# A two-layer cross-attention and mixture-of-experts kernel: attention as straight code, one ring entry for maxima and outputs, stage borders reordered

## The chip, the core and the metric

The kernel runs on one core of one Trainium2 chip. The metric is the time of one execution on the device, in microseconds (us). Its engines are TensorE (PE; PEld is its weight load), VectorE (DVE), ScalarE (ACT), GpSimd (POOL) and SyncE (SP), which here only issues DMAs and waits.

## The reference

Four batches of 512 tokens with 512 features (x), and a context of 512 tokens with 128 features for each batch. Two layers, each of two residual steps with a gate:

```python
x = x + tanh(g_xattn[l]) * attention(layernorm(x), ctx, ctx)   # 32 query heads, 8 kv heads, D = 16
x = x + tanh(g_ffn[l]) * ffn(layernorm(x))
# attention: softmax(q k^T / 4) v, four query heads share a kv head, no projections
# ffn, layer 0: 8 experts of width 256, top 2 by softmax, and a shared expert of width 1024
# ffn, layer 1: 32 experts of width 192, top 6 by sigmoid, and a shared expert of width 384
# an expert: (silu(x wg) * (x wu)) wd; the chosen ones' weights are normalized to sum 1
```

All is float32. The kernel gets its precision on TensorE from splitting each operand into a high and a low part in a shorter type (names in `_hi`, `_lo`, `_parts`) and adding three products.

## The kernel before

x stays in SBUF for the whole program (16 tiles of 128 tokens, L50 and L580 share it). The stages follow each other: attention of layer 0 (0 to 479 us), FFN of layer 0 (to 1042), attention of layer 1 (to 1512), FFN of layer 1 (to 2289). Each stage is a block in which every engine runs its own program, written out by hand, with semaphores between them.

**Attention** (make_attention, L50). A *unit* is one kv head of one batch: 32 units. Each engine has a `step(b, k)`, and `steps` (L100) runs it for batch 0 as straight code, for batches 1 to 3 in a hardware loop (`Fori`), and for four more steps that drain the pipeline. In step n the maxima of unit n - 1 are taken, the negated maxima of n - 2 are turned and placed, unit n - 3 is exponentiated and multiplied by v, and the output of n - 4 is turned and scaled.

- The scores are computed twice. Once (score_for_max, L354) with tokens of x on the partitions: 16 blocks of 128 x 512 for a unit, of which VectorE takes the row maxima (take_max, L528). Then (score_for_exp, L369) with context on the partitions, where one row of the weights holds the maximum, which comes with the product; ScalarE takes the exponential, and probs_times_v (L388) multiplies by v and a column of ones.
- Three PSUM banks, `ring_ps`, are shared in turn (RING_ORDER, RING_BANK, L36 to L47) by 16 score blocks ("max"), the turned maxima ("neg", turn_max L331), the turned x of a later head pair ("q", turn_q L319, odd steps only) and the turned output ("out", turn_out L341). An entry may be written when the one three places before it has been read (ring_bank_free, L296).
- Maxima: POOL splits them in high and low (split_max, L236), TensorE turns them in four transposes of 8 columns, ScalarE copies 8 rows of 512 (copy_max, L443), SyncE places them by DMA in `q_turned` (place_max, L181). The output is copied by ScalarE (copy_out), turned by four transposes, divided by its sum on VectorE (scale_out, L541, after maximum 14) and added to x by POOL.
- Operands of the score matmuls are laid out by SyncE: place (L156) issues seven DMAs for a unit: three parts of k, three of q, and a tile of "no maximum". It waits first for the split of k and of q.
- For each batch VectorE takes mean and variance (moments, L485), subtracts k_hi from the context (split_k, L515) and normalizes (L498). Moments and split_k of batches 1 to 3 stand at the head of steps 1 to 3 of batch 0; the normalization stands among the maxima of step 4 of the batch before (next_batch, L505). POOL has the inverse root (root). In the last four steps the moments for the FFN are taken, a batch each.
- Loads at the start: x of batch 0 in one DMA, the whole transposed context in one, two gates, the context by tokens, and x of batches 1 to 3, all from SyncE (L140 to L154).

**FFN** (make_ffn, L580). VectorE takes the last moments, normalizes 16 tiles (L1281), SyncE stores them as rows in DRAM. A router chooses experts; VectorE makes the entries of a table (one pass for each chosen expert k, L1366 to L1371), then 35 small operations for the schedule (L1373 to L1414). TensorE then runs the shared expert in four groups of 512 tokens: for each of FC blocks of its width a gate/up phase (L969), then a down phase (L996), with y added to x by VectorE (L1492). Between its matmuls it makes the table by one-hot matmuls (L948; tile_hot by VectorE, tile_one_hots L1428, slot_hot by POOL, L813), over a ring of HOTS buffers (three in layer 1, four in layer 0). finish_table (L1445) reads it. Then the routed experts: POOL gathers 128 tokens at a time by indirect DMA (gather, L832), indexed by rows_in (VectorE, L1517), TensorE turns them (turn_x, L1016), multiplies with the expert's weights, and the results are scattered and added. Before: gathers 0 and 1 come after the schedule was read back, ScalarE's first rounding of expert weights after the last y (L1243), and the first expert's low parts (gu_lo) after the table.

The order of the work is that of these hand-written programs. An engine that waits holds back all that stands behind the wait in its program.

## Time and profile before

| | us |
|---|---|
| median of three runs | 2295.39 (2292.28 to 2306.82) |
| the profiled execution | 2291.02 |
| its span | 2289.3 |
| mean granted TensorE clock | 0.958 |
| attention of layer 0, of layer 1 | 479, 470 |
| FFN of layer 0, of layer 1 | 563, 777 |

The stage times are read off the timeline. The span is from the first to the last instruction of the profiled execution; the metric lies 1.7 us above it there. Busy time counts instructions only, not waits. In a timeline row the bracket holds the idle time ahead of it and the instruction that ended it.

### The profile page before, as it was taken

The numbers are of one execution on the slowest core, as the hardware profiler recorded it, in microseconds if no ns is written. First come the engines' busy times: TensorE is split into PE (matmuls) and PEld (weight loads), VectorE is DVE, ScalarE is ACT, GpSimd is POOL, SyncE is SP. The second block draws the span as 40 slices with busy tenths as digits, with TensorE's granted clock in tenths as the row PEclk, the third lists the DMA queues.
The fourth block names the chain that finished last, engine by engine and source line by source line (L and its number), as shares of the span: only waits on it lengthen the run. The fifth ranks groups of instructions, "written<-read, shape, count | busy, mean of one in ns | idle before, by whom it ended". The sixth has DMA issues, their size and how long they took to land. (4 is left out here: it accounts for less than half of the span.)

```text
span 2289.3 us, 42900 instructions
## 1 busy us (share of the span) xinstructions
PE 1990.7 (87%) x10024; PEld 1202.6 (53%) x10025; DVE 1349.5 (59%) x2607; ACT 1114.5 (49%) x1741; POOL 737.8 (32%) x856
## 2 busy tenths in 40 slices
PE   3899999979999979992899999976887998999997
PEld 1333333334666748871333333333555887878776
DVE  5888788833234324433888888838664454454443
ACT  1677676741212215540477777752113555565554
POOL 3111121121201015553121112122662554555555
PEclk9999999999999989995799999998998999999998
DMA  5222222141000037755122222140004787788785
GB/s 166 55 63 53 52 60 56 41 178 44 19 19 1 19 110 180 165 106 176 46 59 60 58 52 57 46 146 10 28 19 132 177 186 176 178 194 192 170 190 102
DMA packets 127292, 219.56 MB, mean 96 GB/s; under 512 B 16738, under 2 KB 58724, under 8 KB 126948
## 3 DMA queue, kind: packets, MB, share of 16 engines
q1 hardware_dynamic: 93412, 138.80, 20.7%
q0 software_dynamic: 33792, 79.71, 17.3%
q8 instruction: 40, 0.66, 0.1%
q14 instruction: 48, 0.39, 0.1%
HBM read 114.64 MB, written 56.63 MB: 75 GB/s over the span
## 5 line engine op out<-in xcount | busy, mean ns | idle before, releaser
L539 DVE TENSOR_REDUCE maxima<-ring_ps 128x1 f32<-128x512 f32 x1024 | 651.7, 685 | 150.3 <-PE ring_ps L366 138.7
L457 ACT ACTIVATE probs<-score_ps 128x1024 f32<-128x1024 f32 x512 | 497.1, 1018 | 79.9 <-PE score_ps L383 78.2
L366 PE MATMUL ring_ps<-k_turned,q_turned 64*128 64x512 f32 x1024 | 427.1, 488 | 95.7 <-DVE maxima L539 51.6
L366 PEld LDWEIGHTS ring_ps<-k_turned,q_turned 64*128 64x128 f32 x1024 | 180.6, 194 | 419.7 <-DVE maxima L539 267.1
L1028 PE MATMUL bank_f<-w_gu_parts_f,xg_T_f 128*128 x1800 | 371.2, 355 | 0.4 <-issue 0.4
L1028 PEld LDWEIGHTS bank_f<-w_gu_parts_f,xg_T_f 128*128 128x128 f32 x1800 | 330.5, 192 | 29.0 <-issue 1.3
L383 PE MATMUL score_ps<-q_turned,k_turned 64*128 64x512 f32 x1024 | 331.1, 450 | 1.6 <-ACT probs L457 1.4
L398 PE MATMUL out_ps<-probs,v_ones 128*32 128x512 f32 x2048 | 278.0, 615 | 0.5
L836 POOL DMA_INDIRECT xg_f<-xh_rows_f,idx_in_f x156 | 159.0, 1019 | 305.1 <-DVE idx_in_f L1517 204.5
L1053 PE MATMUL bank_f<-w_dn_parts_f,hg_T_f 96*128 (+1 forms) x888 | 244.2, 411 | 2.6 <-DVE hg_T_f L1529 1.4
L969 PE MATMUL bank_f<-x_parts_f,w_sh_parts_f 128*128 128x512 f32 x792 | 205.0, 400 | 13.6 <-DVE w_sh_parts_f L1442 13.6
L852 POOL DMA_INDIRECT out_x<-y_tok_f,idx_out_f x111 | 184.1, 1658 | 88.0 <-ACT y_tok_f L1225 36.7
L969 PEld LDWEIGHTS bank_f<-x_parts_f,w_sh_parts_f 128*128 128x128 f32 x792 | 148.8, 190 | 46.7 <-issue 16.3
L1053 PEld LDWEIGHTS bank_f<-w_dn_parts_f,hg_T_f 96*128 96x128 f32 (+1 forms) x888 | 157.9, 190 | 28.7 <-issue 3.4
L267 POOL TENSOR_TENSOR x_res<-x_res,scaled 128x256 f32 (+1 forms) x64 | 47.0, 734 | 390.0 <-DVE scaled L551 389.8
L996 PE MATMUL bank_f<-w_sh_down_f,h_T_f 128*128 128x512 f32 x352 | 156.8, 594 | 12.9 <-DVE h_T_f L1472 7.6
L813 POOL TENSOR_SCALAR slot_hot_f<-count_f_f,slot_of_f 128x128 fp32r<-128x128 f32 x128 | 101.9, 803 | 203.0 <-PE bank_f L948 201.9
L1537 DVE TENSOR_TENSOR h_tok_f<-silu_g_f,bank_f 128x192 f32<-128x192 f32 (+1 forms) x148 | 54.5, 368 | 188.6 <-ACT silu_g_f L1215 170.2
L383 PEld LDWEIGHTS score_ps<-q_turned,k_turned 64*128 64x128 f32 x1024 | 144.8, 190 | 25.1 <-ACT probs L457 13.6
L1016 PE MATMUL bank_f<-ident,xg_f 128*128 128x128 f32 x608 | 96.4, 282 | 55.1 <-DMA xg_f<-xh_rows_f,idx_in_f 51.8
L1505 DVE TENSOR_TENSOR w_gu_parts_f<-w_gu_f,w_gu_parts_f (+2 forms) x80 | 80.6, 1012 | 86.2 <-ACT w_gu_parts_f L1187 86.2
L253 POOL CAST q_hi<-q_raw 128x512 fp32r<-128x512 f32 x36 | 22.1, 613 | 291.7 <-ACT q_raw L438 178.0
(206 smaller groups left out, 2213.2 us busy)
## 6 DMA issues: line engine op xcount, KB each, us to landing
q_turned<-q_hi SPq DMA_DIRECT2D x128, 128.0 KB, 2.6
w_gu_f<-in_L_ffn_wg SPq DMA_DIRECT2D x32, 384.0 KB
w_gu_f<-in_L_ffn_wu SPq DMA_DIRECT2D x32, 384.0 KB
w_dn_f<-in_L_ffn_wd SPq DMA_DIRECT2D x32, 384.0 KB
k_turned<-k_hi SPq DMA_DIRECT2D x128, 64.0 KB, 2.1
q_turned<-q_lo SPq DMA_DIRECT2D x64, 128.0 KB, 2.6
q_turned<-no_max SPq DMA_DIRECT2D x64, 128.0 KB, 2.6
xh_rows_f<-xh_f SPq DMA_DIRECT2D x8, 1024.0 KB, 9.6
```

Of the source, the lines that this page charges most:

```text
L366: pe.matmul(ring(k, "max", i), q_turned[rows, slot, h // 2, c * P:(c + 1) * P], k_turned[rows, slot, :], start=True, stop=True).then_inc(m ...
L383: mm = pe.matmul(score_ps[:, pair, a, :], k_turned[rows, slot, c * P:(c + 1) * P], q_turned[rows, slot, pair, :], start=True, stop=True)
L398: mm = pe.matmul(out_ps[32 * h:32 * h + 32, :], v_ones[:, (k - LAG_EXP) % RING, c, :], probs[:, c % 2, h // 2, h % 2, :], start=(c == 0), ...
L457: act.activation(probs[:, c % 2, pair, :, :], score_ps[:, pair, :, :], ACT.Exp, scale=float(D) ** -0.5).then_inc(exped, 1)
L539: dve.tensor_reduce(maxima[:, par, c, col:col + 1], ring(k, "max", i), AX.X, ALU.max).then_inc(max_taken, 1)
L813: pool.tensor_scalar(slot_hot[:, n % HOTS, :], count_f[:], slot_of[:, i, k:k + 1], None, ALU.is_equal).then_inc(slot_hot_made, 1)
L836: pool.indirect_dma_start(xg[:, half, :], None, xh_rows, bass.IndirectOffsetOnAxis(ap=idx_in[:, half:half + 1], axis=0)).then_inc(gathered ...
L852: pool.indirect_dma_start(acc_rows, bass.IndirectOffsetOnAxis(ap=idx_out[:, half:half + 1], axis=0), y_tok[:, half, :], None, compute_op=A ...
L969: mm = pe.matmul(bank[:, 2 * (n % NBK) + o, :], w_sh_parts[:, o, w_part, d, :], x_parts[:, x_part, d, :], start=(d == 0 and j == 0), stop= ...
L996: mm = pe.matmul(bank[:, 6 + c % 2, :], h_T[:, f, c * P:(c + 1) * P], w_sh_down[:, f, :], start=(f == 0), stop=(f == FC - 1))
L1028: mm = pe.matmul(bank[:, half, 0:2 * F], xg_T[:, half, x_part, d, :], w_gu_parts[:, bass.ds(par, 1), w_part, d, :].rearrange("p a f -> p ( ...
L1053: mm = pe.matmul(bank[:, 2 + half, :], hg_T[:, half, h_part, f, :], w_dn_parts[:, bass.ds(par, 1), w_part, f, :].rearrange("p a f -> p (a ...
```

## The change

1. `steps` is straight code for all four batches in both layers; the bank of the last ring entry is no longer set by hand; the last batch does nothing for a batch behind it.
2. Moments and split_k of the next batch move from the head of steps 1 to 3 of batch 0 into the steps 1 (bn_stats), 2 (aggregates) and 3 (halves of split_k) of every batch but the last, between maxima. POOL's root goes to step 2.
3. "neg" and "out" become one ring entry, "turn", in the place of "neg". The 32 rows of maxima are turned by one transpose; the output by four matmuls that have it as weights and a 0/1 tile `pick` of 68 columns as moving operand, so that only the 17 columns in use of each head come out. VectorE, not ScalarE, copies the maxima (32 x 128 instead of 8 x 512), and scales after maximum 6 instead of 14. Each of the two placing DMAs takes 16 rows of 128 instead of 4 rows of 512.
4. At the start of attention x(0) is loaded by tiles, the context by batches (four DMAs in turn with x), gates by ScalarE's queue. ScalarE rounds only k of batch 0 before the first copies of q. The second q is split by VectorE instead of POOL. SyncE places k and "no maximum" first, and q after its wait.
5. FFN, start: tiles 0 to 3 are normalized before the moments of the last batch.
6. FFN, VectorE: passes 4 and 5 over the chosen experts (layer 1) come after the shared parts, the schedule operations are spread over the updates of x in groups 1 and 2, and one-hots are made two further ahead in the gate/up phases.
7. Border to the routed experts: the first two gathers are issued when the table is there; ScalarE's rounding waits for the split of the shared weights and the last h, not for the last y; gu_lo(0) stands before the last updates of x; TensorE waits for the last update only before turn_h(0); SyncE loads the next expert's weights before the last store. For that w_sh_down of layer 1 gets its own memory.

```diff
-TURN_NEG_AT, TURN_Q_AT, TURN_OUT_AT, SCALE_AT = 2, 5, 6, 14
-COPY_OUT_AT, COPY_NEG_AT, COPY_Q_AT = 1, 3, 6
+USED = D + 1
+TURN_AT, TURN_Q_AT, SCALE_AT = 2, 5, 6
+COPY_OUT_AT, COPY_Q_AT = 1, 6
...
-order += [("neg", 0)] * (d == TURN_NEG_AT) + [("q", 0)] * (d == TURN_Q_AT and k % 2) + [("out", 0)] * (d == TURN_OUT_AT)
+order += [("turn", 0)] * (d == TURN_AT) + [("q", 0)] * (d == TURN_Q_AT and k % 2)
...
-RING_BANK[RING_ORDER[-1]] = 1
...
-def steps(eng, step):
...
-    for k in range(KVH):
-        step(0, k)
-    with eng.Fori(1, B) as b:
+def steps(step):
...
+    for b in range(B):
...
+    def load_ctx_T(b):
+        sp.dma_start(ctx_T[:, :, b * S:(b + 1) * S], t["ctx_T"][:, :, b * S:(b + 1) * S]).then_inc(ctx_T_loaded[b], 16)
...
-    load_x(0)
-    sp.dma_start(ctx_T[:], t["ctx_T"]).then_inc(ctx_T_loaded, 16)
-    for i, g in enumerate((t["g_xattn"], t["g_ffn"])):
-        sp.dma_start(gate_raw[:, i:i + 1], g[layer:layer + 1].rearrange("(a n) -> a n", a=1).to_broadcast([P, 1])
-                     ).then_inc(gate_loaded, 16)
-    sp.dma_start(ctx_tok[:], t["ctx"].rearrange("b (n p) d -> p (b n) d", p=P)).then_inc(ctx_loaded, 16)
-    for b in range(1, B):
-        load_x(b)
+    for c in range(TPB):
+        sp.dma_start(x[:, c, :], t["x_rows"][c * P:(c + 1) * P, :]).then_inc(x_first[c], 16)
+    for b in range(B):
+        load_ctx_T(b)
+        if b == 0:
+            sp.dma_start(ctx_tok[:], t["ctx"].rearrange("b (n p) d -> p (b n) d", p=P)).then_inc(ctx_loaded, 16)
+        else:
+            load_x(b)
...
-        sp.wait_ge(k_lo_made, b + 1)
-        sp.nop(nofuse=True)
-        sp.wait_ge(q_split, b * (KVH // 2) + (2 * (k // 4) + 2))
+        sp.wait_ge(k_lo_made, 2 * b + 2)
...
+        sp.dma_start(q_turned[3:P:4, k, :, :].bitcast(F32), no_max[:]).then_inc(placed[k % 2], 16)
+        sp.wait_ge(q_split, b * (KVH // 2) + (2 * (k // 4) + 1))
+        sp.nop(nofuse=True)
+        if (b, k) == (0, 0):
+            sp.wait_ge(second_q, 2)
+        sp.nop(nofuse=True)
...
-        sp.dma_start(q_turned[3:P:4, k, :, :].bitcast(F32), no_max[:]).then_inc(placed[k % 2], 16)
...
+    pool.memset(pick[:], 0.0).then_inc(picked, 1)
+    pool.wait_ge(picked, 1)
+    pool.affine_select(out=pick[:], in_=pick[:], compare_op=ALU.not_equal, fill=1.0, base=0,
+                       pattern=[[-P // G, G], [-1, USED]], channel_multiplier=1).then_inc(picked, 1)
...
-            elif what == "neg":
+            elif what == "turn":
+                if (u := stage(b0, k0, LAG_OUT)) is not None:
+                    pe.wait_ge(out_read, u + 1)
...
-                    return pe.wait_ge(max_copied, u + 1)
-            elif what == "out":
-                if (u := stage(b0, k0, LAG_OUT)) is not None:
-                    return pe.wait_ge(out_read, u + 1)
-            elif not isinstance(b0, int) or -3 <= b0 * KVH + k0 < UNITS:
+                    pe.wait_ge(max_copied, u + 1)
+                if u is not None or stage(b0, k0, LAG_OUT) is not None:
+                    return
+            elif -3 <= b0 * KVH + k0 < UNITS - 3:
...
-        ring_bank_free(b, k, "neg")
-        for c in range(TPB):
-            mm = pe.transpose(ring(k, "neg")[0:2 * G, c * P:(c + 1) * P].bitcast(F32R),
-                              max_parts[:, (k - LAG_NEG) % 2, c, :], ident_r[:])
-        mm.then_inc(max_turned, 1)
+        ring_bank_free(b, k, "turn")
+        pe.transpose(ring(k, "turn")[0:2 * SLOTS, SLOTS * USED:SLOTS * USED + P].bitcast(F32R),
+                     max_parts[:, (k - LAG_NEG) % 2, :], ident_r[:]).then_inc(max_turned, 1)
...
-        ring_bank_free(b, k, "out")
+        if stage(b, k, LAG_NEG) is None:
+            ring_bank_free(b, k, "turn")
+        if isinstance(b, int) and u == 0:
+            pe.wait_ge(picked, 2)
...
-            mm = pe.transpose(ring(k, "out")[:, c * P:(c + 1) * P], out_rows[:, c * P:(c + 1) * P], ident[:])
+            mm = pe.matmul(ring(k, "turn")[:, c * G * USED:(c + 1) * G * USED], out_rows[:, c * P:(c + 1) * P],
+                           pick[:].rearrange("p h e -> p (h e)"), start=True, stop=True)
...
                 probs_times_v(b, k, c)
-            if d == TURN_NEG_AT:
+            if d == TURN_AT:
                 turn_max(b, k)
+                turn_out(b, k)
             if d == TURN_Q_AT:
                 turn_q(b, k)
-            if d == TURN_OUT_AT:
-                turn_out(b, k)
...
+    round_k(0)
     copy_q(-1, 5)
     copy_q(-1, 7)
-    steps(act, step)
+    for b in range(1, B):
+        round_k(b)
+    steps(step)
...
+    def next_batch(b, k, n):
...
-        if rest:
-            return
-        if c == 0:
-            dve.wait_ge(ln_rstd, B)
-            dve.wait_ge(q_turns, b * (KVH // 2) + KVH // 2)
-        normalize(b + 1 if isinstance(b, int) else (b + 1) % B, c)
...
-    def split_k(b):
+        if b + 1 >= B or rest:
+            return
+        if k == 1:
+            if c == 0:
+                dve.wait_ge(x_loaded[b + 1], 16)
+            moments_of_tile(b + 1, c)
+        elif k == 2 and c == 0:
+            moments_of_batch(b + 1)
+        elif k == 3 and c < 2:
+            split_k(b + 1, c)
+        elif k == KVH // 2:
+            if c == 0:
+                dve.wait_ge(ln_rstd, b + 2)
+                dve.wait_ge(q_turns, b * (KVH // 2) + KVH // 2)
+            normalize(b + 1, c)
...
+    def split_k(b, half):
...
-        dve.tensor_tensor(k_lo[:, :, cols], ctx_T[:, :, cols], k_hi[:, :, cols].bitcast(F32), ALU.subtract
+        dve.tensor_tensor(k_lo[:, half, cols], ctx_T[:, half, cols], k_hi[:, half, cols].bitcast(F32), ALU.subtract
...
-    dve.wait_ge(x_loaded[0], 16)
-    moments(0)
+    def split_second_q():
...
+        dve.wait_ge(q_copied, 2)
+        dve.tensor_copy(q_hi[:, 0, 1, :], q_raw[:, 1, :]).then_inc(second_q, 1)
+        dve.wait_ge(second_q, 1)
+        dve.tensor_tensor(q_lo[:, 0, 1, :], q_raw[:, 1, :], q_hi[:, 0, 1, :].bitcast(F32), ALU.subtract).then_inc(second_q, 1)
...
+    for c in range(TPB):
+        dve.wait_ge(x_first[c], 16)
+        moments_of_tile(0, c)
+    moments_of_batch(0)
...
-    split_k(0)
+    for half in range(2):
+        split_k(0, half)
+    split_second_q()
...
+    def copy_max(b, k):
+        if (u := stage(b, k, LAG_NEG)) is None:
+            return
+        par = (k - LAG_NEG) % 2
+        dve.wait_ge(max_turned, u + 1)
+        if (out := stage(b, k, LAG_OUT)) is not None:
+            dve.wait_ge(out_turned, out + 1)
+        if past(b, k, LAG_NEG + 2):
...
+            dve.wait_ge(max_placed[par], 16 * u + (0 if par == 0 else -16))
+        dve.tensor_copy(max_rows[:, par, :], ring(k, "turn")[0:2 * SLOTS, SLOTS * USED:SLOTS * USED + P]
+                        ).then_inc(max_copied, 1)
...
-        turned_out = ring(k, "out").rearrange("p (c h e) -> p (c h) e", c=TPB, h=G)
+        turned_out = ring(k, "turn")[:, 0:SLOTS * USED].rearrange("p (n e) -> p n e", n=SLOTS)
...
     def step(b, k):
-        if isinstance(b, int) and b == 0 and 0 < k < B:
-            dve.wait_ge(x_loaded[k], 16)
-            moments(k)
-            split_k(k)
-        if isinstance(b, int) and b == B and k >= 1:
+        if b == B and k >= 1:
             dve.wait_ge(x_added, KVH * k)
-            moments(k - 1, B)
+            for c in range(TPB):
+                moments_of_tile(k - 1, c)
+            moments_of_batch(k - 1, B)
         for n in range(SLOTS):
...
             if n == SCALE_AT:
+                copy_max(b, k)
                 scale_out(b, k)
-            if k == KVH // 2:
-                next_batch(b, n)
-    steps(dve, step)
+            next_batch(b, k, n)
+    steps(step)
     dve.wait_ge(x_added, UNITS)
...
+        if b == B - 1:
...
+            sp.wait_ge(expert_w, 48)
+            sp.wait_ge(hot_used, PAIRS)
+            load_expert(1, 1)
...
-    sp.wait_ge(expert_w, 48)
-    sp.wait_ge(hot_used, PAIRS)
-    load_expert(1, 1)
...
+    gather(0, 0)
+    gather(1, 1)
...
-    for i in range(7):
-        if i >= 2:
-            pool.wait_ge(xg_turned, i - 1)
+    for i in range(2, 7):
+        pool.wait_ge(xg_turned, i - 1)
...
     turns = pe.value_load(turns_i[0:1, 0:1], min_val=4, max_val=64)
+    pe.wait_ge(y_read, TT - 1)
     turn_x(0, 0)
...
     gate_up(1, 1, expert_of(1))
+    pe.wait_ge(y_read, TT)
     turn_h(0, 0)
...
-    act.wait_ge(y_done, TT)
+    act.wait_ge(sw_split, 2 * (B - 1) * FC)
+    act.wait_ge(h_done, B * FC)
     gu_hi(0, 0)
     gu_hi(0, 1)
+    if layer == 0:
+        act.wait_ge(y_done, TT)
     dn_hi(0)
...
+    for i in range(TPB):
+        normalize(i)
...
-    for k in range(K):
+    def weights_of(k):
...
+        dve.wait_ge(table_ready, 1)
+        rows_in(0, 0)
+        rows_in(1, 1)
+    for k in range(min(K, 4)):
+        weights_of(k)
     shared_x_lo(1)
...
     shared_w_lo(FC, 1)
+    for k in range(4, K):
+        weights_of(k)
     for n in range(FC, B * FC):
...
             used = hots_by(g, (f * 2 + o + 1) * HC * 3)
-            tile_one_hots(used)
+            tile_one_hots(used + (2 if f + 1 < FC else 0))
             if f + 1 < FC:
                 shared_w_lo(n + 1, o)
-        if f + 1 < FC:
-            tile_one_hots(used + HOTS // 2)
         dve.wait_ge(silu_done, n + 1)
...
+        if g + 1 == B:
+            gu_lo(0, 0)
+            gu_lo(0, 1)
...
+            if (g, c) == (1, 0):
+                experts_ended()
+            if (g, c) == (1, 1):
+                next_expert()
+            if (g, c) == (1, 2):
+                schedule_of()
+            if (g, c) == (1, 3):
+                turn_counts()
+            if (g, c) == (2, 0):
+                last_tokens()
+            if (g, c) == (2, 1):
+                first_tokens()
+            if (g, c) == (2, 2):
+                experts_meet()
+            if (g, c) == (2, 3):
+                landing_counts()
```

## Rows read from the trace of the kernel before

In a fence, "..." stands where lines of the answer are left out.

**Rows 1.** The page, parts 1 and 2: busy time of each engine, and TensorE's granted clock.

```profile
PE 1990.7 (87%) x10024; PEld 1202.6 (53%) x10025; DVE 1349.5 (59%) x2607; ACT 1114.5 (49%) x1741; POOL 737.8 (32%) x856
...
PEclk9999999999999989995799999998998999999998
```

**Rows 2.** Windows: busy (count) of PE, PEld, DVE, ACT, POOL; granted clock; DMA share; GB/s.

```profile
140.00:200.00 60.00, 57.34 (x353) 22.48 (x352) 53.19 (x92) 43.29 (x51) 10.59 (x24) 1.00 0.25 62
...
234.00:236.00 2.00, 2.00 (x10) 1.16 (x7) 0.00 (x0) 0.74 (x2) 0.00 (x1) 0.50 0.49 110
...
22.00:24.00 2.00, 0.00 (x0) 0.00 (x0) 0.00 (x0) 0.00 (x0) 2.00 (x2) 1.00 1.04 383
```

**Rows 3.** Timeline of VectorE, the scaling once a step: start us, busy us, engine, line, operation.

```profile
156.62 0.42 DVE L551 TENSOR_TENSOR scaled<-ring_ps,recip 128x256 f32<-128x256 f32 x1
...
168.60 0.42 DVE L551 TENSOR_TENSOR scaled<-ring_ps,recip 128x256 f32<-128x256 f32 x1
...
181.40 0.42 DVE L551 TENSOR_TENSOR scaled<-ring_ps,recip 128x256 f32<-128x256 f32 x1
...
194.44 0.42 DVE L551 TENSOR_TENSOR scaled<-ring_ps,recip 128x256 f32<-128x256 f32 x1
...
231.81 0.42 DVE L551 TENSOR_TENSOR scaled<-ring_ps,recip 128x256 f32<-128x256 f32 x1
...
250.59 0.42 DVE L551 TENSOR_TENSOR scaled<-ring_ps,recip 128x256 f32<-128x256 f32 x1
...
1273.12 0.42 DVE L551 TENSOR_TENSOR scaled<-ring_ps,recip 128x256 f32<-128x256 f32 x1
...
1287.89 0.43 DVE L551 TENSOR_TENSOR scaled<-ring_ps,recip 128x256 f32<-128x256 f32 x1
```

**Rows 4.** Timeline of TensorE, FFN layers; in brackets idle time before and who ended it.

```profile
839.41 1.12 PE L1016 MATMUL bank_f<-ident,xg_f 128*128 128x128 f32 x4 [10.12 <-DMA xg_f<-xh_rows_f,idx_in_f]
...
1600.06 1.62 PE L969 MATMUL bank_f<-x_parts_f,w_sh_parts_f 128*128 128x512 f32 x3 [13.61 <-DVE w_sh_parts_f L1442]
...
1612.78 0.41 PE L948 MATMUL bank_f<-tile_hot_f,slot_hot_f 128*128 128x384 f32 x1 [1.21 <-DVE tile_hot_f L1421]
...
1740.13 1.11 PE L1016 MATMUL bank_f<-ident,xg_f 128*128 128x128 f32 x4 [8.76 <-DMA xg_f<-xh_rows_f,idx_in_f]
```

**Rows 5.** Timeline of VectorE, the filling of batch 0 in layer 0.

```profile
32.90 2.46 DVE L489 BATCH_NORM_STATS2 stats<-x_res 128x6 f32<-128x512 f32 x4
...
35.89 1.22 DVE L518 TENSOR_TENSOR k_lo<-ctx_T,k_hi 128x1024 fp32r<-128x1024 f32 x1
```

**Rows 6.** Timeline of TensorE, attention of layer 0.

```profile
29.29 0.79 PE L366 MATMUL ring_ps<-k_turned,q_turned 64*128 64x512 f32 x2 [13.19 <-DMA q_turned<-no_max]
...
254.46 0.41 PE L337 MATMUL ring_ps<-ident_r,max_parts 128*8 128x128 f32 x4
...
255.08 0.50 PE L366 MATMUL ring_ps<-k_turned,q_turned 64*128 64x512 f32 x1 [0.21 <-DVE maxima L539]
...
261.22 0.66 PE L347 MATMUL ring_ps<-ident,out_rows 128*128 128x128 f32 x4
```

**Rows 7.** Groups of instructions by line: busy us, mean ns, idle before and releaser.

```profile
L539 DVE TENSOR_REDUCE maxima<-ring_ps 128x1 f32<-128x512 f32 x1024 | 651.7, 685 | 150.3 <-PE ring_ps L366 138.7 <-issue 7.2
...
L813 POOL TENSOR_SCALAR slot_hot_f<-count_f_f,slot_of_f 128x128 fp32r<-128x128 f32 x128 | 101.9, 803 | 203.0 <-PE bank_f L948 201.9
```

**Rows 8.** Timeline of SyncE's queue at the start of attention, layer 0.

```profile
22.75 0.56 SPq L174 DMA_DIRECT2D k_turned<-k_hi  x1
...
26.54 0.60 SPq L179 DMA_DIRECT2D q_turned<-no_max  x1
```

**Rows 9.** Timeline of VectorE in the FFN of layer 1.

```profile
1526.48 1.92 DVE L1288 TENSOR_SCALAR xh_f<-x_res,mean_var,rstd 128x512 f32<-128x512 f32 x4 [7.02 <-DMA xh_rows_f<-xh_f]
...
1586.77 0.18 DVE L1373 CAST ends_i_f<-ends_f_f 128x32 int32<-128x32 f32 x1
...
1597.02 2.28 DVE L1436 TENSOR_TENSOR x_parts_f<-xT_f,x_parts_f 128x2048 fp32r<-128x2048 f32 x1
```

202 lines of the change are left out of this document (103 added, 99 removed).

## Prediction

> **What bounds the kernel now.** I read the page's busy times first. TensorE is busy for 87% of the span and VectorE for 59%, and the granted clock is near full in all but a few slices [rows 1]. So TensorE bounds the kernel, and time can be won only in two ways: give it less to do, or close gaps in it. Next come the windows by stage. In the steady part of an attention layer TensorE is busy for 57.34 of 60 us [rows 2], so 4% is there to win by scheduling. At the edge of the attention loop it runs at half the clock, 0.50 (the 1.2 GHz level), after a pause in which all engines stood still [rows 2]. Then I timed a step (one kv head of one batch) by the spacing of the "scaled" instruction on VectorE: 11.98 us for a plain step, 13.04 us for one with four normalizations among its maxima, 18.78 us at a loop edge of layer 0 and 14.77 us at one of layer 1 [rows 3]. In the FFN layers the gaps stand in the timeline of TensorE: one of 13.61 us before the first shared group of layer 1, small ones of 1.21 us at the table's one-hots, and one of 10.12 and of 8.76 us at the border from shared to routed experts [rows 4]. Two layers, so most items count twice.
>
> **Edges of the loop.** Batches 1 to 3 run in a loop of TensorE, VectorE, ScalarE, POOL and SP; straight code takes its place. Each layer has two jumps back and an exit. In layer 0 the jumps cost 18.78 - 11.98 = 6.8 us each (two of them, alike within 0.01), and the entry and tail another 2.5 together: 16.1. In layer 1 the first jump takes 14.77 [rows 3] and the second is shorter: 2.8 and 1.4, with entry and tail 2.5: 6.7. I take these back in full, **-22**. Below: with the slow-clock microseconds after each pause [rows 2] also back, -28. Above: 0, if straight code stalls for its own instructions. That jumps of one loop differ from 1.4 to 6.8 speaks for a stall of instruction loading, and in straight code the next instructions can be fetched ahead of use.
> The Trainium skill (Runtime: NRT & Kernel Launch, section Instruction fetch mechanics) says that prefetch is purely sequential and that a taken branch outside the loaded window forces a stall. The trace's loop edges agree with it in place; by that rule the term is -22 too.
>
> **The filling of batch 0.** In the first three steps VectorE does a lump before its first maximum: four bn_stats, 2.46 us, four aggregates and a sum, 0.55, and the k_lo subtraction of 1.22, about 4.1 us [rows 5] (of it 0.4 of small waits); TensorE has nothing queued past the three ring banks, so it stands. Three lumps cost the layer some 9.5 us of TensorE time (three times 4.1 less what the filling hid). Spread among the maxima, the same work costs what four normalizations of 0.54 cost today: 13.04 - 11.98 = 1.06 per step [rows 3]. It now falls in batches 0, 1 and 2: statistics in step 1 (+1.3), aggregates in step 2 (+0.3), halves of k_lo in step 3 (+0.5), so +1.9 to 2.1 a batch. For batch 0 that is inside the 9.5; for batches 1 and 2 it is new. -9.5 + 3.9 = -5.6 a layer, **-11**. Bounds -19 (spread work hidden under maxima's waits for TensorE) and 0.
>
> **One ring entry for maxima and outputs.** Today a step has a maxima turn of 0.41 and an output turn of 0.66 overlapping to 0.59, with small waits of 0.21 behind the former [rows 6], so 1.0 of PE time and about 0.3 of stalls. After: one transpose, 0.10, and four fp32 matmuls of 68 columns with the rows as weights. Each is two passes as the 128-column form is (0.66 for four [rows 6]), so 0.14 to 0.21 for each of four: 0.56 to 0.86. Work falls by about 0.3 to 0.5. Against that, one entry of three banks now holds a bank until maximum 6 is read (0.68 [rows 7]), a copy (an estimate of 0.23, half of the 0.42 of the scaling [rows 3], for half the columns), a reciprocal of the same size and the scaling are done: 0.9 us of VectorE in a row where there was 0.7, plus handing over of 0.25. The maximum that wants this bank then waits 0.3 to 0.5. Net I take -0.2 a step, 56 steps: **-11**. The new wait, for both turns, has all later maxima of VectorE behind it, and behind those TensorE; both turns end before maximum 5, so it should cost nothing. Bounds: -0.5 (-28) and +0.3 (+17). VectorE gains 0.23 a step and ScalarE loses 0.59; neither is the bound (53.19 and 43.29 of 60 [rows 2]), but VectorE comes nearer. The negated maxima land 8.7 us into a step: the copy ends at about 5.5, after six of sixteen maxima and the turn, SP issues for 0.56 [rows 8], and from an issue to the score that used it 2.7 us passed at the start (26.54 [rows 8] to 29.29 [rows 6]). They are wanted at about 9.4, where TensorE's first score for exp of that unit stands: hidden, with 0.7 of slack where there was 1.6.
>
> **No work for a fifth batch.** The last batch turns and normalizes nothing: four q turns and the four normalizations, 1.06 + 1.3, -2.4 a layer, **-5**. Bounds -6 and -3.
>
> **Start of attention.** The first score waits 13.19 us for the landing of the last placement [rows 6]: k parts are issued from 22.75 and no_max, the last, at 26.54 [rows 8]. Reordered, the q parts would be issued at about 17.6 (x by tiles, so that statistics, normalization, two turns and two splits start earlier, by as much as three of four tiles of the load). But the loads of x and ctx are still filling the DMA engines at 22 to 24 (383 GB/s [rows 2]) and end near 24.5. The placements, 704 KB, drain behind them in 1.8 us, plus 1 of latency: 27.3 instead of 29.3, **-4** for two layers. Bounds: at once, 17.6 + 2.7 = 20.3, -9 a layer (-18); and +2 a layer, if ctx in smaller pieces (2 KB for 8) makes the loads longer.
> The Trainium skill (DMA: Bandwidth & Descriptors, section Queues, rings and completion order) says that on each DMA engine the descriptors of one issuer's ring are consumed in order. It speaks against this edit: placements issued early stand behind SP's loads. By it the term is -4; without it, -18. No row of before shows a placement issued while a load of the same queue was still waiting.
>
> **Start of the FFN.** Four normalizations move ahead of the last batch's moments. Today VectorE normalizes two batches after the moments and then waits 7.02 us for the stored rows, before four that take 1.92 [rows 9]. What precedes the store (variance, POOL's root, zeroing) is late by the 1.92 of four normalizations: +1.9 twice, **+4**. Bounds 0 (the pause swallows it) and +4.
>
> **Schedule arithmetic of layer 1.** 35 small VectorE instructions from 1586.77 to 1597.02, 10.25 us, stand ahead of the parts that the first shared group waits for [rows 9]. So do two groups of weights, which move only behind those parts (they take some 3 us, and the first one-hots come after them, in good time). They go into the down phases of groups 1 and 2. The gap of 13.61 shrinks by 10.25. But in a down phase VectorE must feed one-hots through a ring that holds three: 4.73 us of arithmetic in group 1 and 5.53 in group 2 come back as waits, 10.26. Net with a little clock **-1**. Bounds -14 (arithmetic hidden under the down phases) and +6. In layer 0 it is hidden before and after: 0.
>
> **One-hots ahead.** In layer 1 TensorE waits 1.21 us for a one-hot at each f border of the gate/up phases [rows 4]: four a group, three groups, 14.4. Asking for two more one-hots before hides nearly all: -13 in layer 1 and -1.3 in layer 0, **-14**. Bounds -16 and 0: POOL's share of a one-hot takes 0.80 us [rows 7], not far from the pace of use, so POOL may be next.
>
> **Borders.** The gathers of the first two tiles are issued from the table instead of after the schedule; gate/up weights no longer wait for the last y. The gaps of 10.12 and 8.76 us [rows 4] close to nothing, as the gather (flight near 7) then lies beside the last down phase: **-19**. Bounds -19 and -5 (the table's last one-hots come at the end of the phase, and some flight stays uncovered).
>
> **Sum.** -22 - 11 - 11 - 5 - 4 + 4 - 1 - 14 - 19 = -83. The profiled execution took 2291.0; 2291 - 83 = 2208. The median of the runs shown lies 4.4 above the profiled one: **2212**.
>
> **Rivals.** (1) The merged turn doesn't pay: VectorE's chain decides, +0.3 a step instead of -0.2: +28, 2240. For it: a chain of copy, reciprocal and scaling on an engine with 53 of 60 us used; against it: PE work falls. Chance 0.17. (2) Placements don't queue behind the loads: -14 more, 2198. For it: 2.7 us of flight in the steady part; against: 383 GB/s on the engines at that time. 0.12. (3) Straight code stalls at its own fetches as often as the loop did: the 22 are not won, 2234. 0.06. (4) Slower than before: the copy of the maxima, now behind both turns and behind maximum 6, makes the negatives land late and all score matmuls for exp wait. From +1.4 us in each of some 60 steps it eats the 83; at +1.6, where -0.2 stood, it gives 2212 + 1.8 x 56 = 2313. For it: slack falls from 1.6 to 0.7 us. Against: a lateness of over 2 us needs a flight of twice the 2.7 seen. 0.05. The forecast itself has 0.60.
>
> **How the numbers follow.** The main case's own range is 2185 to 2238 (its terms at half way to their bounds, signs mixed). To 2240 and 2198 it takes in rivals 1 to 3, and the bounds of the borders and the schedule (+14, -13) widen it to 2180 to 2250. A change of 1% is 23 us, about what a measurement of this kernel can tell from none. Faster by over 1% means under 2272: the main case and rivals 1 to 3 lie there, 0.90 with 0.05 off for a joint miss of several terms; that goes to "within". Slower is rival 4, 0.05.
>
> **What would show it.** Right: steps at 11.8 us (plain) without any of 14 to 18; the clock above 0.95 around 235 us; no lump of four bn_stats; the gap before the first shared group near 3.4, and new waits for one-hots of some 5 us each in the down phases of groups 1 and 2; no waits of 1.2 us at f borders; under 1 us at the borders; the first score at 27.3. The sum is wrong if plain steps are longer than 12.2 us, if TensorE waits for max_rows, or if POOL's one-hots become the releaser in the gate/up phases.

## The result and the profile after

The changed kernel takes 2231.69 us in the median (2225.11 to 2237.43), 0.9723 of the time before, with a 95% interval of 0.9694 to 0.9752. The forecast was 2212 in a range of 2180 to 2250: right in direction and inside the range, 20 us too low. Of the two profiled executions the span fell from 2289.3 to 2227.7, by 61.6 us, where the sum promised 83.

The page after, the lines that answer to [rows 1]:

```profile
PE 1987.7 (89%) x10072; PEld 1224.0 (55%) x10073; DVE 1357.3 (61%) x2675; ACT 1087.7 (49%) x1673; POOL 723.2 (32%) x848
...
PEclk9999999989999999995999999989999999999998
```

TensorE did the same work (1987.7 us against 1990.7) in a shorter span: what was won are gaps. The windows of the changed kernel, in the columns of [rows 2]:

```profile
140.00:200.00 60.00, 56.64 (x352) 23.58 (x348) 54.37 (x102) 41.41 (x46) 13.32 (x27) 1.00 0.25 63
...
232.00:244.00 12.00, 11.56 (x77) 5.07 (x73) 11.46 (x21) 7.57 (x9) 0.60 (x3) 1.00 0.25 61
```

The steady part didn't get denser: 56.64 of 60 us, where it was 57.34 [rows 2]. The stretch around the first former loop edge now runs at a granted clock of 1.00; from 232 to 244 us it was 0.67 before. The step, by the spacing of VectorE's scaling as in [rows 3]:

```profile
203.68 0.42 DVE L593 TENSOR_TENSOR scaled<-ring_ps,recip 128x256 f32<-128x256 f32 x1
...
215.69 0.43 DVE L593 TENSOR_TENSOR scaled<-ring_ps,recip 128x256 f32<-128x256 f32 x1
...
228.84 0.42 DVE L593 TENSOR_TENSOR scaled<-ring_ps,recip 128x256 f32<-128x256 f32 x1
```

A plain step takes 215.69 - 203.68 = 12.01 us, the next, with a q turn before its maximum 6, 228.84 - 215.69 = 13.15. A pair is 25.16, where before it was 24.62 (11.98 from [rows 3], and 12.64 for the step ahead of it, from the row at 143.98 shown below). TensorE in that stretch, and its first score:

```profile
29.01 1.22 PE L379 MATMUL ring_ps<-k_turned,q_turned 64*128 64x512 f32 x3 [14.18 <-DMA q_turned<-q_lo]
...
213.07 1.08 PE L359 MATMUL ring_ps<-pick,out_rows 128*128 128x68 f32 x8
...
216.17 0.49 PE L379 MATMUL ring_ps<-k_turned,q_turned 64*128 64x512 f32 x1 [0.37 <-DVE scaled L593]
...
221.13 0.50 PE L396 MATMUL score_ps<-q_turned,k_turned 64*128 64x512 f32 x2 [0.42 <-ACT probs L465]
```

Four output matmuls of 68 columns are eight passes that take 1.08 us, not 0.56 to 0.86; the four transposes of 128 columns in [rows 6] are four passes (x4), and not two each, as the prediction has it. The maximum behind the merged entry waits 0.37 us for the scaling. In the step with a q turn there is a new wait of 0.42 for ScalarE's exponential. The first score comes at 29.01, not at the 27.3 forecast. In the FFN layers, TensorE again:

```profile
806.94 0.60 PE L1060 MATMUL bank_f<-ident,xg_f 128*128 128x128 f32 x4
...
1547.92 0.66 PE L994 MATMUL bank_f<-tile_hot_f,slot_hot_f 128*128 128x384 f32 x1 [5.47 <-DVE tile_hot_f L1497]
...
1579.95 0.41 PE L994 MATMUL bank_f<-tile_hot_f,slot_hot_f 128*128 128x384 f32 x1 [2.81 <-DVE tile_hot_f L1497]
...
1624.75 0.41 PE L994 MATMUL bank_f<-tile_hot_f,slot_hot_f 128*128 128x384 f32 x1 [3.60 <-DVE tile_hot_f L1497]
...
1717.02 0.66 PE L1060 MATMUL bank_f<-ident,xg_f 128*128 128x128 f32 x4 [4.09 <-DMA xg_f<-xh_rows_f,idx_in_f]
```

At 806.94 (layer 0's border) the first turn has no wait any more; before it was 10.12 [rows 4]. Behind it TensorE now waits 2.72 us for VectorE's part of the turned rows (xg_T; 2.29 in layer 1), where it was 1.56. The first shared group of layer 1 now waits 5.47 us, for a one-hot, in the place of 13.61 [rows 4]. The longest waits for a one-hot in the down phases of groups 1 and 2 are 2.81 and 3.60. Before there was one in the same place, of 1.47 and 1.48:

```profile
1636.61 0.41 PE L948 MATMUL bank_f<-tile_hot_f,slot_hot_f 128*128 128x384 f32 x1 [1.47 <-DVE tile_hot_f L1421]
```

Added up over a down phase, these waits grew from 2.9 to 6.0 us in group 1 and from 2.9 to 8.2 in group 2. The waits of 1.2 at the f borders are gone. 4.09 us are spent waiting for a later gather.

**Where the 61.6 us went**, by the times at which the same TensorE instruction stands in both traces: the start of both attention layers gave 0.3 and 1.3; from the first score to the last turn of the maxima layer 0 fell from 431.1 to 407.9 and layer 1 from 421.6 to 408.2, so 36.6; the FFN starts cost 3.1 in layer 0 and gave 1.0 in layer 1; the shared groups gave 1.8 in layer 0 and 9.6 in layer 1; the borders gave 8.6 and 8.7, of which layer 1 returned 3.2 in its routed part. 1.6 + 36.6 - 2.1 + 11.4 + 14.1 = 61.6.

### The profile page after: what moved, and what is told of

Read it like the earlier page. It is cut to its first block and busy times, and to the rows that moved or that the text cites. A ratio compares the mean times of both kernels' runs of the same rounds, so it can differ in the third digit from the quotient of the medians.

```text
span 2227.7 us, 40122 instructions
## 1 busy us (share of the span) xinstructions
PE 1987.7 (89%) x10072; PEld 1224.0 (55%) x10073; DVE 1357.3 (61%) x2675; ACT 1087.7 (49%) x1673; POOL 723.2 (32%) x848
## 5 line engine op out<-in xcount | busy, mean ns | idle before, releaser
L465 ACT ACTIVATE probs<-score_ps 128x1024 f32<-128x1024 f32 x512 | 503.1, 1025 | 214.5 <-PE score_ps L396 212.5
L379 PE MATMUL ring_ps<-k_turned,q_turned 64*128 64x512 f32 x1024 | 412.8, 481 | 62.0 <-DMA q_turned<-q_lo 27.1
L1042 PE MATMUL bank_f<-w_sh_down_f,h_T_f 128*128 128x512 f32 x352 | 162.9, 613 | 12.6 <-DVE h_T_f L1567 7.6
L396 PEld LDWEIGHTS score_ps<-q_turned,k_turned 64*128 64x128 f32 x1024 | 149.6, 186 | 37.8 <-ACT probs L465 28.8
L278 POOL TENSOR_TENSOR x_res<-x_res,scaled 128x256 f32<-128x256 f32 x64 | 47.1, 735 | 240.1 <-DVE scaled L593 240.1
```

The costliest lines, as they stand in the source:

```text
L379: pe.matmul(ring(k, "max", i), q_turned[rows, slot, h // 2, c * P:(c + 1) * P], k_turned[rows, slot, :], start=True, stop=True).then_inc(m ...
L396: mm = pe.matmul(score_ps[:, pair, a, :], k_turned[rows, slot, c * P:(c + 1) * P], q_turned[rows, slot, pair, :], start=True, stop=True)
L465: act.activation(probs[:, c % 2, pair, :, :], score_ps[:, pair, :, :], ACT.Exp, scale=float(D) ** -0.5).then_inc(exped, 1)
L1042: mm = pe.matmul(bank[:, 6 + c % 2, :], h_T[:, f, c * P:(c + 1) * P], w_sh_down[:, f, :], start=(f == 0), stop=(f == FC - 1))
```

## The experiments

Times are medians; the ratio is to runs of the kernel before on the same chip. The changed kernel stands at 2231.69, 0.9723.

**straight_only.** The kernel before, with one part of the change.

```diff
-            for k in range(KVH):
-                step(0, k)
-            with eng.Fori(1, B) as b:
+            for b in range(B):
                 for k in range(KVH):
                     step(b, k)
```

> The kernel before with its attention loop written as straight code and nothing else changed (a batch that does not exist is still prepared). Theory (the loop's edges are instruction loading and registers): the steps at the edges, 18 us and 15 us, fall to those of the middle, the span falls by 22 us from 2289 to 2267. Rival (straight code stalls at its own fetches): under 5 us are won.

Measured 2287.49, ratio 0.9960 (0.9933 to 0.9986): 9 us, not 22. The trace tells why. TensorE at the first border of batches (a wait, then the turns of the maxima on either side of it, which lie 9 us before and 5 us after the wait):

```profile
131.35 0.49 PE L364 MATMUL ring_ps<-k_turned,q_turned 64*128 64x512 f32 x1 [1.13 <-DVE scaled L549]
...
122.11 0.41 PE L335 MATMUL ring_ps<-ident_r,max_parts 128*8 128x128 f32 x4
...
136.13 0.40 PE L335 MATMUL ring_ps<-ident_r,max_parts 128*8 128x128 f32 x4
```

From 122.11 to 136.13 is 14.02 us in straight code. The kernel before has the same wait at the same border, where no jump is, as it enters the loop:

```profile
131.06 0.50 PE L366 MATMUL ring_ps<-k_turned,q_turned 64*128 64x512 f32 x1 [1.14 <-DVE scaled L551]
```

In the prediction's own measure, VectorE's scaling, it shows as a step of 13.40 us at that border, 1.4 over the plain 11.98:

```profile
130.58 0.43 DVE L551 TENSOR_TENSOR scaled<-ring_ps,recip 128x256 f32<-128x256 f32 x1
...
143.98 0.42 DVE L551 TENSOR_TENSOR scaled<-ring_ps,recip 128x256 f32<-128x256 f32 x1
```

So of the 18.78 us at a loop edge 1.4 had nothing to do with the loop. In four of the eight borders of straight_only the granted clock also falls to 0.50 (1.2 GHz) behind this wait, and the step takes 15.10 to 15.18 us instead of 14.02. At the third border of layer 0:

```profile
336.00:338.00 2.00, 2.00 (x12) 1.32 (x8) 0.90 (x2) 1.07 (x2) 0.00 (x0) 0.50 0.59 139
```

Layer 1 of the kernel before has no more than this at its jumps: its steps there take 15.35 us (with the clock at 0.50 behind the wait) and 13.96 by the turns of the maxima. Its loop cost nothing that these rows show. In layer 0 each jump cost some 5.2 us: the step over it and the one behind take 18.02 + 13.31 by the same turns, in straight code 14.02 + 12.07. The part that belongs to the loop is seen on VectorE at the first edge of the kernel before, an idle time that no other engine ends ("issue"):

```profile
239.08 3.08 DVE L539 TENSOR_REDUCE maxima<-ring_ps 128x1 f32<-128x512 f32 x5 [2.28 <-issue]
```

Straight code removed this one; neither expectation had the split right.

**ring_runs_on.** straight_only, with the three banks counted on from batch to batch.

```diff
-RING_BANK[RING_ORDER[-1]] = 1
+RING_LENGTH = len(RING_ORDER)
...
-            return ring_ps[:, RING_BANK[k, what, i], :]
+            return ring_ps[:, (RING_BANK[k, what, i] + b * RING_LENGTH) % 3, :]
...
-                    if RING_BANK[k0, what, i] != RING_BANK[RING_ORDER[at]]:
+                    if back % 3:
```

> The kernel of straight_only with the ring's banks counted on through the batches, so that every entry reuses the bank of the entry three before it; before, the order of 148 entries began anew in each batch with bank 0, and the last output stood in bank 1. Theory (TensorE's wait of 1.13 us for the scaling at each end of a batch comes from this wrap, not from the loop): the steps of 14.02 us fall to 12.65, eight of them, so the span falls by about 11 us against straight_only, and about 20 against the kernel before (0.991). Rival (what is left at the batch borders is instruction loading): as straight_only, 0.996.

Measured 2271.73, ratio 0.9887 (0.9828 to 0.9947), 16 us below straight_only, 17 by the ratios. The wait is gone, and the step over the border takes 134.63 - 121.97 = 12.66 us:

```profile
121.97 0.40 PE L335 MATMUL ring_ps<-ident_r,max_parts 128*8 128x128 f32 x4
...
134.63 0.40 PE L335 MATMUL ring_ps<-ident_r,max_parts 128*8 128x128 f32 x4
```

The theory holds, and the gain is larger than the 11 us that it named. Eight steps shorter by 1.36 give 10.9, and the four that lost 1.1 us each to the clock give another 4.6: no border step of this trace is over 12.67. The order of 148 entries began anew with each batch, and its last entry, maximum 15, was put by hand into bank 1, where the output two entries ahead of it still stood until VectorE's scaling. The merged entry takes the place of that output far from the end of the order; its 140 entries begin anew too, but there a bank is only waited for behind a maximum, and no such wait is left in the changed kernel. The change names it in half a sentence (the bank of the last entry is no longer set by hand), and the prediction gives it no term. Against sep_turns, below, which keeps that bank, three border steps a layer are shorter by 0.87 and the last by 1.4, which makes 8 us of the gain.

**sep_turns.** The changed kernel with two ring entries again.

```diff
-TURN_AT, TURN_Q_AT, SCALE_AT = 2, 5, 6
-COPY_OUT_AT, COPY_Q_AT = 1, 6
+TURN_NEG_AT, TURN_Q_AT, TURN_OUT_AT, SCALE_AT = 2, 5, 6, 14
+COPY_OUT_AT, COPY_NEG_AT, COPY_Q_AT = 1, 3, 6
```

(with the two turns, copy_max of ScalarE, 8 rows of 512, and bank 1 for the last entry as in the kernel before)

> The changed kernel with maxima and outputs turned in two ring entries again, the maxima copied by ScalarE, the scaling after maximum 14; all else as changed. Theory (the merged entry costs time): a pair of steps takes 24.65 us as before the change instead of 25.16, about 14 pairs a layer, so the span falls by about 14 us, to 2214. Rival (the prediction's term, merging gains 0.2 us a step): the span rises by 11 us, to 2239.

Measured 2246.40, ratio 0.9773 (0.9729 to 0.9818): 0.005 or 11 us slower than the changed kernel, as the prediction's term says and not as the theory made from the trace. The two intervals overlap, but the traces say the same: between the first and the last turn of the maxima the two layers take 17.2 us more, of which 6.1 fall on four steps with the clock at half, and 11.0 are left. Yet its steps are the faster ones (the turn of the maxima in the last batch):

```profile
363.15 0.41 PE L342 MATMUL ring_ps<-ident_r,max_parts 128*8 128x128 f32 x4
...
375.22 0.41 PE L342 MATMUL ring_ps<-ident_r,max_parts 128*8 128x128 f32 x4
...
387.89 0.40 PE L342 MATMUL ring_ps<-ident_r,max_parts 128*8 128x128 f32 x4
```

12.07 + 12.67 = 24.74 for a pair, 0.42 less than 25.16. What it loses is at the borders of batches, 14.02 there as above, and in the steps with statistics and normalization, which are 0.6 and 0.8 us longer; why these two are longer is not shown. Without the places where the clock dips in one of the traces, a batch in the middle takes 104.03 us here and 102.08 in the changed kernel.

**copy_q_later** and **scale_earlier**, each one number of the changed kernel.

```diff
-COPY_OUT_AT, COPY_Q_AT = 1, 6
+COPY_OUT_AT, COPY_Q_AT = 1, 7
```

> The changed kernel with ScalarE's copy of the turned q behind its exponential 7 instead of 6. Theory (the copy waits for the turn and holds back exponential 7, for which TensorE then waits 0.42 us): the step with a q turn takes 12.7 us instead of 13.15, the span falls by 10 to 12 us. Rival (VectorE's chain sets the step): the wait moves to the ring, no change.

Measured 2217.25, ratio 0.9639 (0.9597 to 0.9681): 14 us by the medians. ScalarE now has both exponentials behind it when the turned q comes:

```profile
217.43 1.94 ACT L465 ACTIVATE probs<-score_ps 128x1024 f32<-128x1024 f32 x2 [1.07 <-PE score_ps L396]
...
220.06 0.60 ACT L456 ACTIVATE q_raw<-ring_ps 128x512 f32<-128x512 f32 x1 [0.69 <-PE ring_ps L338]
```

The step with a q turn takes 12.59 instead of 13.15.

```diff
-TURN_AT, TURN_Q_AT, SCALE_AT = 2, 5, 6
+TURN_AT, TURN_Q_AT, SCALE_AT = 2, 5, 5
```

> The changed kernel with copy_max and scale_out of VectorE after maximum 5 instead of 6. Theory (VectorE stands 0.46 us before maximum 6 while the turn is done, and TensorE waits 0.35 us for the scaling behind it): the plain step falls from 12.01 to about 11.65, the span by some 18 us. Rival (the bank of the next maximum comes free later by as much, or VectorE waits for the turn itself): no change or slower.

Measured 2207.34, ratio 0.9589 (0.9544 to 0.9633): 24 us for one number. The plain step takes 11.58 instead of 12.01. The scaling ends before maximum 6 is read, in the time in which VectorE used to stand, and the score behind the merged entry has no wait:

```profile
200.69 0.42 DVE L593 TENSOR_TENSOR scaled<-ring_ps,recip 128x256 f32<-128x256 f32 x1
...
202.05 0.81 PE L379 MATMUL ring_ps<-k_turned,q_turned 64*128 64x512 f32 x2
```

So the forecast's doubt about the merged turn (VectorE's chain of copy, reciprocal and scaling holds the bank) was sound; the chain stood one maximum too late.

**lump_again.** The changed kernel with the moments at the head of steps 1 to 3 of batch 0.

```diff
             def step(b, k):
+                if b == 0 and 0 < k < B:
+                    dve.wait_ge(x_loaded[k], 16)
+                    for c in range(TPB):
+                        moments_of_tile(k, c)
+                    moments_of_batch(k)
+                    for half in range(2):
+                        split_k(k, half)
...
```

(the same pieces taken out of the later steps, and POOL's root with them)

> The changed kernel with the moments and the split of k of batches 1 to 3 at the head of steps 1 to 3 of batch 0 again. Theory of the prediction: 9.5 us a layer come back in batch 0, 3.9 are saved in the later ones, so the span rises by 11 us to 2239. Rival (the spread work is hidden among the maxima and costs next to nothing): it rises by 16 to 19 us.

Measured 2253.11, ratio 0.9798 (0.9739 to 0.9857): 21 us more by the medians, 17 by the ratios (the interval touches that of the changed kernel; the traces below are clear). The turns of unit 0, of unit 7 and of unit 15, first here, then in the changed kernel:

```profile
54.66 0.29 PE L347 MATMUL ring_ps<-ident_r,max_parts 128*32 128x128 f32 x1
...
147.90 0.23 PE L347 MATMUL ring_ps<-ident_r,max_parts 128*32 128x128 f32 x1
...
249.00 0.23 PE L347 MATMUL ring_ps<-ident_r,max_parts 128*32 128x128 f32 x1
```

```profile
48.58 0.29 PE L347 MATMUL ring_ps<-ident_r,max_parts 128*32 128x128 f32 x1
...
136.48 0.22 PE L347 MATMUL ring_ps<-ident_r,max_parts 128*32 128x128 f32 x1 [0.19 <-DVE maxima L568]
...
238.56 0.23 PE L347 MATMUL ring_ps<-ident_r,max_parts 128*32 128x128 f32 x1 [0.20 <-DVE maxima L568]
```

The first turn comes 6.1 us later, the next seven units take 5.3 more, so the lumps cost 11.4 a layer and not 9.5. The second batch takes 101.10 instead of 102.08: spreading costs 1.0 a batch and not 1.95. That the statistics fill VectorE's waits for scores is the likely reason, not shown by itself. The rival's size holds: 9.4 a layer.

**loads_later.** The changed kernel's loads moved.

```diff
-            for b in range(B):
-                load_ctx_T(b)
-                ...
-                    load_x(b)
+            load_ctx_T(0)
...
                 place_max(b, k)
+                if (b, k) == (0, 1):
+                    for later in range(1, B):
+                        load_ctx_T(later)
+                        load_x(later)
```

> The changed kernel with SyncE's loads of context and x of batches 1 to 3 issued behind the placements of units 0 and 1. Theory (placements are served in the order of issue behind the loads on the same queue, they land 7.5 us after their issue instead of 2.7): the first score comes at 23.5 us instead of 29.0, the span falls by about 5 us a layer, to 2217. Rival (the operands or the engines are late anyway): the first score stays near 29, no change; a second rival, that the batches behind come late: VectorE waits for x in step 1.

Measured 2235.32, ratio 0.9723 (0.9668 to 0.9779): no change. But the two rows of theory and second rival are both there. In the changed kernel SyncE issues the placements of unit 0 from 15.12 on, and the last at 21.48 (the second of two rows; the first is held for 3.14):

```profile
15.12 3.14 SPq L176 DMA_DIRECT2D k_turned<-k_hi  x1
...
21.48 0.59 SPq L185 DMA_DIRECT2D q_turned<-q_lo  x1
```

The first score stands at 29.01, 7.5 us behind. With the loads out of the way SyncE issues the last at 18.99, and TensorE starts 2.7 us later:

```profile
18.99 0.59 SPq L181 DMA_DIRECT2D q_turned<-q_lo  x1
```

```profile
21.68 1.22 PE L379 MATMUL ring_ps<-k_turned,q_turned 64*128 64x512 f32 x3 [6.67 <-DMA q_turned<-q_lo]
...
34.20 1.39 PE L379 MATMUL ring_ps<-k_turned,q_turned 64*128 64x512 f32 x2 [7.78 <-DVE maxima L568]
```

So placements do stand behind loads issued earlier on the same queue, by 4.8 us here. The packets show that they wait and are not merely slowed: those of 4,096 bytes, which in this stretch only the placements have, start at 25.09 in the changed kernel, though the first DMA that has them was issued at 19.57, and at 17.36 with the loads out of the way, 1.3 us after their issue at 16.11. This is what the Trainium skill (DMA: Bandwidth & Descriptors, section Queues, rings and completion order) says of descriptors in a ring, and the runs agree. SyncE itself is held too: its first placement takes 3.14 us to issue behind the loads, 0.54 without them. The 7.3 us won were then lost at once in step 1, where x of batch 1 is late:

```profile
32.86 0.69 DVE L496 BATCH_NORM_STATS2 stats<-x_res 128x6 f32<-128x512 f32 x1 [7.28 <-DMA x_res<-in_x]
```

**ffn_passes_later.** The changed kernel with two moves on VectorE.

```diff
-            for k in range(4, K):
-                weights_of(k)
             for n in range(FC, B * FC):
...
+                if f == FC - 1 and g < 3 and 3 + g < K:
+                    weights_of(3 + g)
                 dve.wait_ge(silu_done, n + 1)
...
+                    if (g, c) == (1, 0):
+                        experts_ended()
+                    ...
                     dve.wait_ge(y_done, TPB * g + c + 1)
```

> The changed kernel with the passes over the fifth and sixth chosen expert in the last gate/up phase of groups 1 and 2, and the pieces of the schedule ahead of VectorE's wait for y instead of behind the update. Theory (the one-hots come in the order of the chosen experts, so the first ones don't need these passes, for which TensorE now waits 5.47 us; the pieces fit into VectorE's waits of 1.4 us): the wait of 5.47 goes, those of 2.81 and 3.60 us fall by half, the span falls by 8 us to 2219. Rival (VectorE is the bound of these groups): the waits turn up at the f borders and the time stays.

Measured 2215.02, ratio 0.9641 (0.9587 to 0.9695): 17 us, where the theory had 8. TensorE at the first gate/up phase, and its waits in the two down phases:

```profile
1546.35 1.25 PE L1015 MATMUL bank_f<-x_parts_f,w_sh_parts_f 128*128 128x512 f32 x3
...
1577.48 0.41 PE L994 MATMUL bank_f<-tile_hot_f,slot_hot_f 128*128 128x384 f32 x1 [2.69 <-DVE tile_hot_f L1497]
...
1619.24 0.41 PE L994 MATMUL bank_f<-tile_hot_f,slot_hot_f 128*128 128x384 f32 x1 [3.42 <-DVE tile_hot_f L1497]
```

The wait of 5.47 is gone. The two in the down phases stayed, 2.69 and 3.42: VectorE makes the low part of x for the next group ahead of the one-hot, as it did in the kernel before (1.47), and a piece of the schedule still stands there too, five operations from 1574.91 to 1576.05 in group 1. The shorter waits behind these fell, and the sum over a down phase went from 6.0 to 4.3 and from 8.2 to 6.0.

Much of the rest is the clock. Windows of the second down phase (group 2), here and in the changed kernel:

```profile
1611.60:1634.50 22.90, 16.95 (x53) 9.40 (x54) 20.84 (x42) 1.70 (x3) 14.42 (x15) 1.00 0.05 16
```

```profile
1616.90:1645.00 28.10, 19.90 (x51) 10.63 (x52) 20.84 (x42) 2.09 (x3) 13.30 (x15) 0.88 0.00 1
```

Over the three shared groups the stretch takes 119.4 us instead of 135.3: 6.2 less of waits and 7.4 less of TensorE's busy time for the same instructions, at a granted clock of 0.99 instead of 0.92.

**border_again.** The changed kernel with the border as before (gathers after the schedule, the expert's weights after the last y, TensorE's wait ahead of the first turn).

```diff
-            gather(0, 0)
-            gather(1, 1)
             pool.wait_ge(sched_in, 16)
...
-            act.wait_ge(sw_split, 2 * (B - 1) * FC)
-            act.wait_ge(h_done, B * FC)
+            act.wait_ge(y_done, TT)
...
-            pe.wait_ge(y_read, TT - 1)
+            pe.wait_ge(y_read, TT)
...
```

> The changed kernel with the border to the routed experts as before: gathers 0 and 1 after the schedule, gate/up weights of the first expert after the last y and the table, TensorE's wait for the last update ahead of the first turn. (The store order of SyncE and the memory of w_sh_down stay changed.) Theory: the gaps of 10.1 and 8.8 us are back, of which the trace of the changed kernel saves 8.6 and 8.8, and a later gather of layer 1 gives 3.2 back to it; the span rises by 14 to 17 us, to 2243. Rival (the gathers are bound by the rows of the DMA engines over the whole stage): under 8 us.

Measured 2243.82, ratio 0.9761 (0.9713 to 0.9808): 12 us by the medians, 9 by the ratios, where the theory had 14 to 17. The intervals overlap; the waits are clear:

```profile
814.75 1.09 PE L1059 MATMUL bank_f<-ident,xg_f 128*128 128x128 f32 x4 [6.55 <-DMA xg_f<-xh_rows_f,idx_in_f]
...
1689.24 1.09 PE L1059 MATMUL bank_f<-ident,xg_f 128*128 128x128 f32 x4 [7.17 <-DMA xg_f<-xh_rows_f,idx_in_f]
```

6.55 and 7.17 us are waited for the first gather, less than the 10.12 and 8.76 of before; SyncE's changed order of stores stayed in, and whether the difference is due to it wasn't tried.

**best_a** is the changed kernel with scale_earlier, copy_q_later and ffn_passes_later, and with the loads so:

```diff
                 place_max(b, k)
+                if (b, k) == (0, 0):
+                    load_x(1)
+                if (b, k) == (0, 1):
+                    load_ctx_T(1)
+                    for later in range(2, B):
+                        load_ctx_T(later)
+                        load_x(later)
```

> The changed kernel with scale_earlier (scaling after maximum 5), copy_q_later, ffn_passes_later, and the loads: x of batch 1 behind the placement of unit 0, all others behind that of unit 1. Theory: -24 (scaling, measured), -17 (passes, measured), part of the -14 of the q copy (the same wait may be shared), -6 a layer from the start, as x of batch 1 no longer comes late: the span falls to about 2165 (ratio 0.945). Rival (the waits of scaling and q copy are one): 2180.

Measured 2175.14, ratio 0.9458 (0.9415 to 0.9502). TensorE has its first score at 21.73, and no wait for the maxima as long as the 7.78 of loads_later:

```profile
21.73 1.22 PE L382 MATMUL ring_ps<-k_turned,q_turned 64*128 64x512 f32 x3 [6.78 <-DMA q_turned<-q_lo]
...
27.27 1.39 PE L382 MATMUL ring_ps<-k_turned,q_turned 64*128 64x512 f32 x2 [0.79 <-DVE maxima L571]
```

A new wait came instead, of 3.42 us (4.56 in layer 1). ScalarE rounds k of batches 1 to 3 ahead of its first copy of q in the steps, and now waits for the last piece of the context:

```profile
37.43 1.06 ACT L448 ACTIVATE k_hi<-ctx_T 128x1024 fp32r<-128x1024 f32 x1 [3.11 <-DMA ctx_T<-in_ctx_T]
```

```profile
39.02 1.22 PE L382 MATMUL ring_ps<-k_turned,q_turned 64*128 64x512 f32 x3 [3.42 <-ACT q_raw L459]
```

The gains of the scaling and of the q copy nearly add: a plain step takes 11.58, one with a q turn 12.16.

**best_b** is best_a with the low part of x moved down.

```diff
                     tile_one_hots(used + HOTS)
-                    shared_x_lo(g + 1)
...
-                    if g + 1 < B and c < 2:
-                        shared_w_lo(n + 1, c)
+                    if g + 1 < B and c == 1:
+                        shared_x_lo(g + 1)
+                    if g + 1 < B and c >= 2:
+                        shared_w_lo(n + 1, c - 2)
```

> best_a with the low part of x of the next shared group and of its first weights made by VectorE among the second to fourth down column instead of before the first. Theory (TensorE waits 2.69 and 3.42 us for the one-hot behind that subtraction): -4 us against best_a. Rival (the subtraction is then late for the one-hots of the next columns): no change or slower.

Measured 2175.98, ratio 0.9469 (0.9417 to 0.9521): no change. TensorE's longest waits in the two down phases became 1.87 and 3.05, at the next column. The wait moved with the subtraction, as the rival has it.

## Why the prediction was right, and which steps of it were not

The total is in part luck: the loop was priced 13 us too high, the filling 6 to 10 too low, and the merged entry came to its number by other parts than those named.

- **Edges of the loop, -22: wrong step, measured -9.** The step that failed is to count all that a border has over 11.98 us as the loop's. By the scaling, the border into the loop took 13.40 without any jump, the wrap of the ring; the second jump of layer 1 took the same 13.40, and the first 14.77, the wrap with the clock at half behind it (straight code has 14.52 for that). So the 6.7 us of layer 1 were none of the loop's, and in layer 0 some 5.3 of the 6.8 a jump were. The prediction counted the wrap as entry and tail of the loop too. That jumps of one loop differ "from 1.4 to 6.8" is then no sign of the size of a stall: in layer 1 nothing is left to explain.
- **Filling, -11: right mechanism, too small.** Lumps 11.4 for 9.5, spreading 1.0 for 1.95 a batch; 17 to 21 us in all. The price of the spread work was taken from the step with normalizations, 1.06 us over the plain one.
- **Merged entry, -11: the sum right (11 by sep_turns) by luck, its parts not.** The matmuls with 68 columns take 1.08 where 0.56 to 0.86 was estimated from columns; a pair of a q turn step and a plain one got 0.42 us longer (ten such pairs, +4). The borders of batches (-8) and the steps with extra work on VectorE (about -7) got shorter by more. Rival 1 named the engine (VectorE's chain holding a bank) and nearly the price (+0.3 a step; it was +0.2 in these pairs), and the total came out the other way by the borders and those steps.
- **No fifth batch, -5:** the last batch's steps 5 and 7 take 12.0 instead of 12.6 in the changed trace, and no normalization stands there. The prediction drops four q turns a layer; the transposes of x went from 144 to 128, which is two a layer. Not tested alone.
- **Start, -4: the queue was seen rightly, measured -1.6.** The first score comes 7.5 us after the last placement's issue, at 29.01 and not at 27.3. The loads end later than before: from 24 to 26 us the DMA engines are busy at a share of 1.06 with 404 GB/s, where it was 0.69 with 207. The prediction has longer loads as a bound (+2 a layer) and does not count them. (That no row of before shows a placement issued while a load was waiting is doubtful: its first one is issued at 22.75 [rows 8], while the engines are full until 24 [rows 2].) Rival 2 (not behind the loads) is refuted for this kernel.
- **FFN start, +4:** +3.1 and -1.0 by the traces. Half right.
- **Schedule and one-hots, -15: measured -11.4.** "In good time" was the failed sentence: the two passes moved behind the shared parts were waited for, 5.47 us. Part of the arithmetic was paid back in the down phases as forecast (3.1 and 5.2 us more of waits, for 4.73 and 5.53). In layer 1 the waits of the shared groups fell by 13.0 us, and 4.4 us were lost again as TensorE's busy time grew with the granted clock down from 0.95 to 0.92. The prediction put the clock down as a small gain.
- **Borders, -19: measured -14,** 12 by border_again. Both gaps closed; behind the first turn a wait grew from 1.56 to 2.72 and 2.29, and 3.2 us came back at a later gather.
- **Rival 3** (straight code stalls): no such stall was found in the straight attention of any trace: outside start and end no idle time over 0.5 us of PE, DVE, ACT or POOL is put down to "issue" there. **Rival 4** (late maxima, slower) had no sign: in the changed kernel TensorE waits for max_rows twice, 0.37 us each, at the first merged entry of a layer.

The single terms in attention (9, 11, 17 to 21 and 5, that is 42 to 46) add to more than the 36.6 seen between the traces. What the parts share wasn't separated, and stays open.
